# A four-layer graph network: one mix product split into high and low parts, a new order on every queue, and no loop

## The reference, cut to what matters

```python
deg = jnp.sum(adj, axis=-1, keepdims=True)
xg = x * jax.nn.sigmoid(deg * Wd[:, 0] + bd)
QK = jax.nn.sigmoid(xg @ Wqk.T + bqk)
scores = jnp.einsum('bnd,bmd->bnm', QK, QK) / math.sqrt(D)
scores = scores * adj
attn = scores / (jnp.sum(scores, axis=-1, keepdims=True) + 1e-06)
out = jnp.einsum('bnm,bmd->bnd', attn, xg)          # the mix
out = out @ Wl.T + bl + xg @ Wr.T
return jax.nn.relu(out)
```

## Time and profile before

| | |
|---|---|
| median of the runs | 1863.97 us |
| profiled execution / its span | 1869.18 / 1867.4 us |
| PE busy | 1804.8 us (97%) |
| DVE busy | 1564.4 us (84%) |
| ACT busy | 1222.0 us (65%) |
| POOL busy | 871.8 us (47%) |
| mean granted TensorE clock | 0.991 |
| HBM traffic | 80.48 MB read, 16.78 MB written, 52 GB/s |

### The profile page before, as it was taken

The page is one execution under the profiler, slowest core; times in us unless marked ns, Lnnn a source line. Parts: engine busy times, 40 slices in busy tenths (PEclk is TensorE's granted clock), DMA queues, the critical chain, the costliest instruction groups (busy, mean ns, idle before and its releaser), DMA issues. The chain is left out here.

```text
span 1867.4 us, 50850 instructions
## 1 busy us (share of the span) xinstructions
PE 1804.8 (97%) x14472; PEld 1580.2 (85%) x14472; DVE 1564.4 (84%) x4444; ACT 1222.0 (65%) x2384; POOL 871.8 (47%) x1807
## 2 busy tenths in 40 slices
PE   5799999999999999999999999999999999999985
PEld 4678888888888888888888888888888888888874
DVE  4678888888888888888888888888888888888874
ACT  3556666676676676676676666667667667667653
POOL 1335445444544544544544544544454454454443
PEclk9899999999999999999999999999999999999998
DMA  4111112112112112112111111211211211211101
GB/s 152 38 41 58 35 58 62 42 51 62 47 45 62 48 45 62 55 37 62 62 31 62 62 34 59 62 42 51 62 48 45 62 48 45 62 55 37 40 29 34
DMA packets 99487, 97.68 MB, mean 52 GB/s; under 512 B 8320, under 2 KB 90368, under 8 KB 99200
## 3 DMA queue, kind: packets, MB, share of 16 engines
q1 hardware_dynamic: 99456, 97.29, 16.7%
HBM read 80.48 MB, written 16.78 MB: 52 GB/s over the span
## 5 line engine op out<-in xcount | busy, mean ns | idle before, releaser
L419 ACT ACTIVATE x<-res,shift,rstd 128x256 f32<-128x256 f32 x512 | 278.5, 594 | 84.8 <-DVE res L900 65.6
L405 POOL TENSOR_SCALAR edge_m<-edge_n 128x2 f32<-128x2 f32 x64 | 14.2, 222 | 483.1 <-issue 470.3
L615 DVE BATCH_NORM_STATS2 stats<-res 128x6 f32<-128x256 f32 x512 | 191.7, 416 | 0.3
L980 PE MATMUL psum<-wk_hi,xT_hi 128*128 128x258 f32 (+1 forms) x512 | 185.9, 363 | 3.4 <-DVE xT_lo L610 3.4
L319 POOL TENSOR_TENSOR rstd<-var_eps,minus_half 128x2 f32<-128x2 f32 x256 | 178.1, 696 | 20.1
L347 POOL TENSOR_TENSOR x_rest<-x,b_half 128x512 f32<-128x512 f32 x64 | 81.7, 1277 | 221.3 <-DVE res L661 221.3
L980 PE MATMUL psum<-wk_hi,xT_lo 128*128 128x258 f32 (+1 forms) x512 | 173.7, 339 | 0.0
L631 DVE TENSOR_TENSOR masked<-psum,adjT 128x512 f32<-128x512 f32 x256 | 163.9, 683 | 11.3 <-PE psum L1043 3.4
L980 PE MATMUL psum<-wk_lo,xT_hi 128*128 128x258 f32 (+1 forms) x512 | 173.0, 338 | 0.0
L578 ACT ACTIVATE z<-hid_relu,hid_bias,hid_rstd 128x512 f32<-128x512 f32 x128 | 97.5, 808 | 107.3 <-POOL hid_bias L384 107.3
L980 PE MATMUL psum<-w_hi,zT_hi 128*128 128x256 f32 x512 | 144.3, 282 | 2.3 <-DVE zT_lo L610 1.2
(11 more groups left out here) (180 smaller groups left out, 6009.4 us busy)
## 6 DMA issues: line engine op xcount, KB each, us to landing
adjT<-in_adj_t SPq DMA_DIRECT2D x256, 128.0 KB, 2.2
xt_in<-in_xt SPq DMA_DIRECT2D x64, 256.0 KB, 2.9
x<-in_x SPq DMA_DIRECT2D x64, 256.0 KB, 2.7
out<-x SPq DMA_DIRECT2D x64, 256.0 KB, 2.3
wts<-in_adj SPq DMA_DIRECT2D x64, 128.0 KB, 2.2
wts<-in_w SPq DMA_DIRECT2D x1, 1028.0 KB, 7.4
wts<-in_w SPq DMA_DIRECT2D x1, 1024.0 KB, 12.2
wts<-in_w SPq DMA_DIRECT2D x1, 769.0 KB, 9.4
```

Source lines behind the costliest of these rows:

```text
L405: pool.tensor_scalar(edge_m[:, :], edge_n[:, :], 1.0, 1.0, ALU.max, ALU.mult).then_inc(sem("edge_0"), 1)
L419: last = act.activation(xs[k + 1][:, g, :], res[k][:, g, :], ACT.Identity, scale=rstd[k][:, g:g + 1], bias=shift[k][:, g:g + 1])
L615: last = dve.bn_stats(stats[k][:, g, :], res[k][:, g, :])
L980: last = pe.matmul(dst, a, r, start=b == 0 and j == 0, stop=b == len(lhs) - 1 and j == 2)
```

## The change: what it does

**The mix as a split product.** `scores` gets a high part `s_hi` (ACT) and a low part `s_lo` (POOL). The right half of `rz` is written as `z3_hi` (ACT, from PSUM) and `z3_lo` (DVE, from PSUM minus `z3_hi`), its left half still as `rz3`. So ACT's two copies of 128x512 become four of 128x256, and one more is added. PE's fp32 product of 128x257 per graph becomes three fp32r products of 128x258.

**No loop.** All 71 turns are written out; counts are numbers, and a wait that an earlier wait on the same engine has already covered is left out (`met`). `claim` waits only on the last holder of a bank.

**Order and banks.** All five lists are put in another order, `TENANTS` gets other banks, and the lists begin at another place of the cycle (most stages of DVE and ACT move by one turn number). On PE `gram` and `xT2` stand before `hid_0`, and `mix_1` before `heads`; the rest keeps its order. On DVE `gate_arg` moves behind the reads of the mix, and `edge_n` in front of `res0`; the two `z3_lo` stand between the reads of `hid_0` and `hid_1`. `gram` and `hid_1` now share a bank, as do `mix_1` and `zT_1`. `pxT` and `att_1` still do.

**Loads.** The weights of L1, L2 and L3 are loaded in turns 1 and 2 instead of turn 0, behind the first adjacency. `x4` and `res3` lie in the space of L3's weights.

The core of the diff:

```diff
-        rz3 = sb("rz3", [P, G, 2 * D + 1])
+        rz3 = sb("rz3", [P, G, D])
+        s_hi, s_lo = sb("s_hi", [P, G, P], F32R), sb("s_lo", [P, G, P], F32R)
+        z3_hi, z3_lo = sb("z3_hi", [P, G, D + 2], F32R), sb("z3_lo", [P, G, D + 2], F32R)
...
+        met = {}
         def wait(eng, name, count, unit=1):
...
-            value = count.times(unit, less)
-            if value is not None:
+            value = unit * count - less
+            if count > 0 and value > met.get((eng, whole), 0):
+                met[eng, whole] = value
                 eng.wait_ge(sem(name), value)

         def turns(eng, turn):
-            for i in range(STAGES - 1):
-                turn(eng, Turn(eng, i))
-            if PAIRS > STAGES - 1:
-                with eng.Fori(STAGES - 1, PAIRS) as i:
-                    turn(eng, Turn(eng, i))
-            for i in range(max(PAIRS, STAGES - 1), TURNS):
+            for i in range(TURNS):
                 turn(eng, Turn(eng, i))
...
 (POOL)
+                if on[6]:
+                    wait(pool, "mix_1", p[6])
+                    wait(pool, "s_hi", n[6])
+                    pool.tensor_tensor(s_lo[:, :, :], scores[:, :, :], value(s_hi[:, :, :]), ALU.subtract) \
+                        .then_inc(sem("s_lo"), 1)
                     wait(pool, "rz_read_1", n[6])
                     pool.tensor_tensor(rz3[:, :, 0:D], rz3[:, :, 0:D], rows(bl_bc), ALU.add).then_inc(sem("r_bias"), 1)
...
 (ACT, in the order xT2_hi, tanh_1, then graph 1 of rz)
-                    act.activation(rz3[:, 0, 0:2 * D], ps("rz_0"), ACT.Copy).then_inc(sem("rz_read_0"), 1)
-                    act.activation(rz3[:, 1, 0:2 * D], ps("rz_1"), ACT.Copy).then_inc(sem("rz_read_1"), 1)
+                    act.activation(z3_hi[:, 0, 0:D], ps("rz_0")[:, D:2 * D], ACT.Copy).then_inc(sem("z3_hi_0"), 1)
+                    act.activation(rz3[:, 0, :], ps("rz_0")[:, 0:D], ACT.Copy).then_inc(sem("rz_read_0"), 1)
...
+                    act.activation(z3_hi[:, 1, 0:D], ps("rz_1")[:, D:2 * D], ACT.Copy).then_inc(sem("z3_hi_1"), 1)
+                    act.activation(rz3[:, 1, :], ps("rz_1")[:, 0:D], ACT.Copy).then_inc(sem("rz_read_1"), 1)
...
+                if on[6]:
+                    wait(act, "scores", n[6])
+                    hi(s_hi[:, :, :], scores[:, :, :], "s_hi")
...
 (DVE, between hidden(0) and hidden(1))
+                    wait(dve, "rz_read_0", n[6])
+                    lo(z3_lo[:, 0, 0:D], ps("rz_0")[:, D:2 * D], value(z3_hi[:, 0, 0:D]), "z3_lo_0")
+                    wait(dve, "rz_read_1", n[6])
+                    lo(z3_lo[:, 1, 0:D], ps("rz_1")[:, D:2 * D], value(z3_hi[:, 1, 0:D]), "z3_lo_1")
...
 (PE)
             def mix_of(g, t, n):
-                wait(pe, "scores", n)
-                claim(f"mix_{g}", t, (f"rz_read_{g}", n))
-                pe.matmul(ps(f"mix_{g}")[:, 0:D + 1], scores[:, g, :], rz3[:, g, D:2 * D + 1],
-                          start=True, stop=True).then_inc(sem(f"mix_{g}"), 1)
+                wait(pe, "s_lo", n)
+                claim(f"mix_{g}", t, (f"z3_lo_{g}", n))
+                split_product(ps(f"mix_{g}")[:, 0:D + 2], [(s_hi[:, g, :], s_lo[:, g, :])],
+                              [(z3_hi[:, g, :], z3_lo[:, g, :])], f"mix_{g}")
```

More of the change, by code:

```diff
@@ L449, in turn @@
                         .then_inc(sem("xcT_read"), 1)
-                if on[2]:
-                    wait(act, "pxT", p[2])
-                    wait(act, "x1_rest", p[2])
-                    normalise(0, n[2])
                 if on[0]:
@@ L458, in turn @@
                     hi(xT0_hi[:, :, :, :], xt_in[:, :, :, :], "xT0_hi")
+                if on[2]:
+                    wait(act, "pxT", p[2])
+                    wait(act, "x1_rest", p[2])
+                    normalise(0, n[2])
                 if on[5]:
@@ L495, in turn @@
                     last.then_inc(sem("qk_tanh"), 1)
-                if on[1]:
-                    wait(act, "headsT", p[1])
-                    wait(act, "masked_3", n[1])
-                    act.activation(att[:, 2:4, :, :, :], masked[:, 2:4, :, :, :], ACT.Tanh).then_inc(sem("tanh_1"), 1)
                 if on[4]:
@@ L655, in turn @@
                     lo(wp_lo[:, :, :], wp_f[:, :, :], value(wp_hi[:, :, :]), "wp_lo")
+                if on[5]:
+                    wait(dve, "hop2", p[5])
+                    wait(dve, "y12_read_1", n[5])
+                    wait(dve, "rows_1", n[5])
+                    _, in_order = both("hop1_0", "hop1_1", slice(D, D + 1))
+                    for g in range(G):
+                        at = g if in_order else G - 1 - g
+                        dve.scalar_tensor_tensor(out=hop1[:, g, :], in0=ps(f"hop1_{g}")[:, 0:D],
+                                                 scalar=row_r[:, at:at + 1], in1=y12[:, g, 0:D],
+                                                 op0=ALU.mult, op1=ALU.add).then_inc(sem(f"hop1_read_{g}"), 1)
@@ new lines, in turn @@
+                if on[1]:
+                    mask(2, n[1], p[1])
+                    mask(3, n[1], p[1])
+                if on[2]:
+                    wait(dve, "prop_read", n[2])
+                    dve.tensor_scalar(deg_m[:, :].unsqueeze(2), degrees(), 1.2e-38, None, ALU.max) \
+                        .then_inc(sem("deg_inv_0"), 1)
+                if on[5]:
+                    wait(dve, "res2", p[5])
+                    wait(dve, "y0_bias", n[5])
+                    wait(dve, "hop2", n[5])
+                    _, in_order = both("hop1_0", "hop1_1", slice(D, D + 1))
+                    for g in range(G):
+                        at = g if in_order else G - 1 - g
+                        last = dve.scalar_tensor_tensor(out=hop2[:, g, :], in0=ps("hop2")[:, g * D:(g + 1) * D],
+                                                        scalar=row_r[:, at:at + 1], in1=y0[:, g, 0:D],
+                                                        op0=ALU.mult, op1=ALU.add)
+                    last.then_inc(sem("hop2_read"), 1)
+                    wait(dve, "x3", p[5])
+                    wait(dve, "hop2_read", n[5])
+                    dve.scalar_tensor_tensor(out=res[2][:, :, :], in0=hop2[:, :, :], scalar=0.0, in1=xs[2][:, :, :],
+                                             op0=ALU.max, op1=ALU.add).then_inc(sem("res2"), 1)
@@ new lines, in turn @@
+                if on[6]:
+                    wait(dve, "res3", p[6])
+                    wait(dve, "r_bias", n[6])
+                    wait(dve, "attn_1", n[6])
+                    _, in_order = both("mix_0", "mix_1", slice(D, D + 1))
+                    for g in range(G):
+                        at = g if in_order else G - 1 - g
+                        dve.scalar_tensor_tensor(out=mix[:, g, :], in0=ps(f"mix_{g}")[:, 0:D],
+                                                 scalar=att_r[:, at:at + 1], in1=rz3[:, g, 0:D],
+                                                 op0=ALU.mult, op1=ALU.add).then_inc(sem(f"mix_read_{g}"), 1)
@@ new lines, in turn @@
+                if on[6]:
+                    aggregate(3, n[6], p[6])
+                if on[1]:
+                    wait(dve, "prop", p[1])
+                    wait(dve, "edge_1", n[1])
+                    for g in range(G):
+                        last = dve.tensor_scalar(inc_b[:, g, 0:P], inc[:, g, :], edge_r[:, g:g + 1], None, ALU.mult)
+                    last.then_inc(sem("inc_b"), 1)
+                if t.first(1):
+                    dve.wait_ge(sem("w2_hi"), 1)
+                    lo(w2_lo[:, :, :], w2_f[:, :, :], value(w2_hi[:, :, :]), "w2_lo")
@@ L1061, in turn @@
                     last.then_inc(sem("pxT"), 1)
+                if t.first(2):
+                    pe.wait_ge(sem("beta_bc"), 1)
+                    claim_once("y1_0", t)
+                    for k in range(NK):
+                        last = pe.matmul(ps("y1_0")[:, 0:D], beta_bc[:, k, :], w2_raw[:, k, :], start=k == 0, stop=k == NK - 1)
+                    last.then_inc(sem("beta_turned"), 1)
                 if on[6]:
```

682 lines of the change are left out of this document (307 added, 375 removed), and 17 rows, old and new, of the table TENANTS.

## The result

The kernel after the change took 1861.68 us (median of 20 runs, 1856.86 to 1863.12), the kernel before 1864.54 us on the same chip (20 runs, 1860.88 to 1870.81). The ratio is 0.9975 with a 95% interval of 0.9967 to 0.9982: 4.7 us faster, between 3.4 and 6.2. The two medians by themselves lie only 2.9 us apart, so the size is known roughly. The forecast was 9.0 us. The sign was right, half of the size or more was missing.

The account below looks back on a forecast made before the run. PE was taken to bound the loop. 57 x (0.16 + 0.09 - 0.04) = 12.0, plus 0.5 for dense turns, less 3.5 for emptying: 9.0 us gained, median 1863.97 to 1855 us; range 1840 to 1885.

Parts of the forecast that it names:

- The mix: On PE, six fp32r products (0.72 us) replace two fp32 products (0.88 us): gain 0.16 us per turn.
- The loop: PE from hop1_0 to hop2: 3.52 us with the jump, 3.43 without, so writing out gains 0.09 us per turn.
- nothing keeps it waiting: In the loop PE, busy 699.90 of 700 us, is the bound and doesn't wait.
- My bound of 0.15 us: Between hop1_0 and hop2: no more than 0.15 us per turn can go while masks start where they do.
- The rival of the costlier jump: All 0.30 us between masks and pxT goes: 12 us more gained, 1843 us; chance 0.12.
- The new order: Reordered lists keep PE's sequence nearly the same; late results at zT_0 or zT_1 cost 0.04 us per turn, range 0 to 0.7.
- A late DVE: Rival: DVE late every turn, 0.25 us at zT_0 or zT_1: 12 us back, 1867 us (1893 with 0.7); chance 0.22.
- the lower end that I had worked out (17.7): z on ACT would end 17.7 to 18.9 us after hop1_0 starts, against 18.2 when PE reaches zT_0.
- `edge_w` held by POOL: Rival: DVE's edge_w waits for POOL's x1_rest, on average 0.64 us, in the chain to z: 1889 us; chance 0.15.
- Record lengths: Rival: by record lengths the six mix products take longer than the two replaced: 28 us slower, 1892; chance 0.04.
- Emptying: Last turns: the mix's longer chain loses 3.5 us (0.8 last, 1.7 before, 0.5 in each of two ahead), bounds 0 and 7.
- Filling: First turns and moved loads: taken at 0, bounds -4 and +4 us.

Follow-up runs that it names:

- the run with the free bank: Kernel after, with pxT in a bank that no mask holds (bank 6) and the degree read from ACT's copy of prop: 1846.66 us, ratio 0.9895.
- written out, covered waits out: Kernel before with all 71 turns written out and every wait already covered by an earlier one on the same engine left out: 1866.89 us, ratio 0.9994.
- same bank, in the kernel before: Kernel before, loop kept, with pxT in a bank that no mask holds (bank 1, behind prop): 1879.41 us, ratio 1.0075.
- the run in the old order: Kernel after, but from turn 64 on r_bias stands ahead of s_lo on POOL and gate_arg ahead of the mix reads on DVE: 1864.26 us, ratio 0.9988.

## Why the prediction was half right

*The mix.* Right in the new order: 0.16 us forecast, 0.15 measured between the change with and without the split. In the old order the same six products gained nothing; why their first one takes longer there stays open.

*The loop.* This step failed, and with it the sentence that it starts from, that in the loop "nothing keeps it waiting". PE's records fill the row of busy time even where PE waits, as the run with the free bank showed. I took 0.09 us per turn from a comparison with turn 64, where masks 0 and 1, as the prediction put it, "already start 0.40 us ahead of `hop1_0` in both places". In the changed kernel the gain is nothing (3.54 for 3.52). The runs give the four cases of the stretch from `hop1_0` to `hop2`:

| | `pxT` waits for masks | `pxT` waits for none |
|---|---|---|
| jump | 3.52 (before) | 3.52 (same bank, in the kernel before) |
| no jump | 3.54 (after), 3.53 (written out, covered waits out) | 3.30 (free bank) |

Jump and masks end within 0.06 us of each other: with the jump alone `pxT` starts 1.19 us after `hop1_0`, with the masks alone 1.13, with neither 0.97. Whoever removes one has the other. My bound of 0.15 us held, but the masks didn't stay where they were. DVE in the kernel after:

```profile
1015.37 1.29 DVE L636 TENSOR_TENSOR masked<-psum,adjT 128x512 f32<-128x512 f32 x2 [0.23 <-PE psum L1046]
```

It waits 0.23 us for `att`, and the mask starts 0.30 us ahead of `hop1_0`, not 0.40. The new order isn't what moved it: in the two runs with the old order written out the mask starts 0.31 us ahead as well. In all these kernels DVE's wait for `att` ends 1.19 to 1.20 us after the start of `att`. In the loop the mask itself carries that wait and starts then (1024.26 - 1023.07 in the kernel before); written out, the wait stands in an instruction of its own, and the mask starts 0.10 us behind it (1015.37 - 1014.08 = 1.29 in the kernel after). Of the 0.16 us by which `pxT` starts earlier at turn 64 than in the loop (1.03 for 1.19 us after `hop1_0`) these 0.10 were lost so. The remaining 0.06 us went into `pxT`: where it starts from a wait, its products take 0.88 us to the next start, where not, 0.81 (1025.85 to 1026.66 in the loop). This could have been seen in the earlier trace rows, where `pxT` to `hop2` is 2.40 us for 2.33 in the earlier trace rows. The total of 3.43 us holds it, but it says that a start from the wait isn't free. The step that failed is the start of the masks, which I took as fixed.

The rival of the costlier jump was right about its price and wrong about the time: 0.2 us are there, hidden. I had set it aside because no instruction packet shows in the loop; the branch's 208 ns on PE were in the same trace. The Trainium skill, page "Runtime: NRT & Kernel Launch", section "Instruction fetch mechanics", has execution stop at a taken branch out of the current window. The longer branch on PE agrees with a stop there, though no packet does, so what those 208 ns are spent on stays open.

*The new order.* I took 0.04 us of waiting per turn; order and writing out cost 0.05 (27.77 for 27.71). 0.15 - 0.05 is what a turn gained, where the forecast had 0.21: 5.3 us in 57 turns for 12.0. None of the results that I had weighed there comes late. ACT's `z` and DVE's mix reads, DVE's `edge_w` (`inc_b` in the row) and POOL's `hid_nm` in the turn from 1015.67:

```profile
1031.63 1.53 ACT L424 ACTIVATE z<-hid_relu,hid_bias,hid_rstd 128x512 f32<-128x512 f32 x2 [1.39 <-POOL hid_bias L361]
```

```profile
1024.61 0.15 DVE L772 TENSOR_TENSOR inc_b<-adjT,ones 128x2 f32<-128x2 f32 x1
...
1033.17 0.87 DVE L851 SCALAR_TENSOR_TENSOR vec<-psum,att_r,rz 128x256 f32<-128x256 f32 x2
```

```profile
1024.97 1.29 POOL L323 TENSOR_TENSOR x_rest<-x,b_half 128x512 f32<-128x512 f32 x1
...
1030.35 0.19 POOL L355 TENSOR_TENSOR hid_nm<-hid_mv,minus_one 128x2 f32<-128x2 f32 x1
```

`z` ends 17.49 us into the turn and PE needs it at 18.38: 0.9 us to spare, a little under the lower end that I had worked out (17.7). A late DVE is refuted here and came true only in the old order with the split. `hid_nm` fell from 0.44 to 0.19 us, as worked out.

*`edge_w` held by POOL.* Didn't happen, by 0.2 us: it ended at 1024.76, and `x1_rest` started at 1024.97. The mechanism is real; `node_r` shows it above, at 1.07 us. The Trainium skill, page "SBUF — State Buffer", section "SBUF: two separate sides", says that the one that starts first holds the ports for its whole instruction; that `node_r`, started 0.07 us after `x_rest`, ends with it agrees.

*Record lengths.* Refuted: six products at 0.12 us.

*Emptying.* 3.5 us forecast, 3.5 measured, for partly other reasons. The last turn lost 1.2 us from `scores` to `att_s` (2.87 for 1.65), and the one before 1.2 too; the run in the old order shows that this is the split's own chain (`scores`, `s_hi`, `s_lo`) and not `r_bias`. `gate_arg` cost 0.5 to 0.6 us, not 0.86.

*Filling.* Forecast 0; 4 to 6 us were gained between the profiles compared above. The loads aren't it; the profiles of kernels in the new order lie at 184.6 to 186.4 us, of those in the old one at 183.3 to 191.0. As these overlap, what in the order does it stays open, and so does how much of it is the spread of single profiles. The averages are 188.0 us for the six of the old order and 185.3 for the seven of the new, 2.7 us apart; 5.3 + 2.7 - 3.5 = 4.5 us comes near the 4.7 that the timed runs say. Here luck helped: with the filling turns as forecast, 5.3 - 3.5 = 1.8 us would be left of the 9.0.

## What to carry to other kernels

Before a stall is counted as gained, list everything that the next instruction waits for, and when each would be met: the two here, which end within a tenth of a microsecond, were worth nothing one by one. The pair is found by removing both. An engine that is busy for the whole of a stretch by its row may still wait, where its records overlap. A wait can be taken away by giving the late tile another bank, and that was worth about three times the whole change here.

## What was not expected of the hardware

Waits that are long met cost time: 0.2 us per turn, with 1725 instead of 299 instructions that only wait in PE's queue in 554 us. A wait that stands in an instruction of its own lets the mask start 0.10 us later than one that the mask carries itself. A branch taken on PE lasts 208 ns, on the other engines 45 to 56. And a 128x2 product on DVE took 1.23 us instead of 0.16 when its second operand moved from PSUM to SBUF beside a POOL instruction.
